# Stage boundaries of a three-layer graph network kernel: who clears the buffers, when a product and a scan start, who stores the last rows

## The reference

```
edge_index = stack([src, dst])
h = maximum(layernorm(x), 0)
x = x + gat(h)                      # 4 heads of 256, self loops, softmax over a node's edges
    # xp = h @ W; e = leaky_relu(a_src[src] + a_dst[dst]); alpha = softmax per target
    # relu(segment_sum(xp[src] * alpha, dst) + bias)
h = maximum(layernorm(x), 0)
x = x + sage2(h)                    # two layers, each:
    # h @ W_self + (segment_sum(h[src], dst) / deg) @ W_neigh + b; relu after the first
```

## Time and profile before

| | us |
|---|---|
| median of 3 runs | 3345.1 (3342.63 to 3353.91) |
| profiled execution | 3346.46 |
| its span | 3344.8 |
| PE busy | 2967.8 (89%) |
| VectorE busy | 2337.4 (70%) |
| ScalarE busy | 1209.0 (36%) |
| GpSimd busy | 1554.0 (46%) |

### The profile page before, as it was taken

One profiled execution on the slowest core, in us unless ns is written; L12 is line 12 of the kernel. 1 busy time (PEld: TensorE's weight loads), 2 busy tenths in 40 slices (PEclk: granted clock), 3 DMA queues, 4 the chain that ended last, 5 costly groups with the idle time before them and its releaser, 6 DMA issues. The chain is left out here.

```text
span 3344.8 us, 64541 instructions
## 1 busy us (share of the span) xinstructions
PE 2967.8 (89%) x20467; PEld 1731.9 (52%) x20467; DVE 2337.4 (70%) x3892; ACT 1209.0 (36%) x2576; POOL 1554.0 (46%) x1534
## 2 busy tenths in 40 slices
PE   4568998499999996999799999997799999997998
PEld 4345665388888885444244444443344444443454
DVE  8787898699999997788466666664455555554343
ACT  3553452588888885444122222222000000001111
POOL 2002232377777773222466666661466656561000
PEclk6788999799999998999899999998899999998999
DMA  3987994498888888777799999994999999996544
GB/s 98 280 274 254 326 354 139 136 324 311 321 305 314 314 317 273 218 218 221 257 345 352 340 351 350 361 358 164 310 350 332 326 346 339 335 356 214 139 134 123
DMA packets 275335, 934.78 MB, mean 279 GB/s; under 512 B 46699, under 2 KB 47719, under 8 KB 275136
## 3 DMA queue, kind: packets, MB, share of 16 engines
q0 software_dynamic: 210560, 713.00, 60.5%
q1 hardware_dynamic: 64576, 219.26, 21.0%
HBM read 852.95 MB, written 130.57 MB: 294 GB/s over the span
## 5 line engine op out<-in xcount | busy, mean ns | idle before, releaser
L1666 PE MATMUL gagg_sum_ps<-gagg_got,gagg_hot_hi 128*128 128x256 f16 x3520 | 591.3, 273 | 78.6 <-ACT gagg_hot_hi L1632 31.3
L1632 ACT ACTIVATE gagg_hot_hi<-gagg_hot,all_mem 128x128 f16<-128x128 f16 x1760 | 538.0, 388 | 138.9 <-DVE gagg_hot L1574 138.9
L1551 POOL DMA_INDIRECT gagg_got<-xs_rows,all_idx x440 | 501.0, 1139 | 179.2 <-issue 132.3
L1726 POOL DMA_INDIRECT agg_got<-h_rows,all_run_idx x415 | 411.8, 992 | 340.1 <-PE agg_sum_ps L1784 198.6
L2072 POOL DMA_INDIRECT agg_got<-h_rows,all_run_idx x415 | 419.1, 1010 | 255.2 <-PE agg_sum_ps L2225 147.7
L1666 PE MATMUL gagg_sum_ps<-gagg_got,gagg_hot_lo 128*128 128x256 f16 x1760 | 481.6, 274 | 0.0
L1758 DVE TENSOR_TENSOR sums_acc<-agg_sum_ps,sums_acc 125x1024 f32 x220 | 269.3, 1224 | 292.3 <-PE agg_sum_ps L1784 290.6
L2136 DVE TENSOR_TENSOR sums_acc<-agg_sum_ps,sums_acc 125x1024 f32 x220 | 269.0, 1223 | 228.8 <-PE agg_sum_ps L2225 227.7
L1784 PE MATMUL agg_sum_ps<-agg_got,agg_hot 128*128 128x512 f16 x1660 | 396.4, 381 | 23.6 <-DMA agg_got<-h_rows,all_run_idx 14.0
L2225 PE MATMUL agg_sum_ps<-agg_got,all_mem 128*128 128x512 f16 x1660 | 392.5, 383 | 24.0 <-DVE all_mem L2106 16.7
L1666 PEld LDWEIGHTS gagg_sum_ps<-gagg_got,gagg_hot_hi 128*128 128x128 f16 x3520 | 329.5, 98 | 122.0 <-ACT gagg_hot_hi L1632 53.3
(11 more groups left out here) (336 smaller groups left out, 4013.2 us busy)
## 6 DMA issues: line engine op xcount, KB each, us to landing
gatw_piece<-slot_rows POOLq DMA_DIRECT2D x56, 512.0 KB, 11.3
split_w<-edg_w_out SPq DMA_DIRECT2D x32, 512.0 KB, 9.4
agg_got<-h_rows,all_run_idx POOLq DMA_INDIRECT x830, 8.0
x_rows<-fin_val POOLq DMA_DIRECT2D x25, 500.0 KB
h_rows<-fin_h POOLq DMA_DIRECT2D x25, 500.0 KB
out_dram<-neigh_rows POOLq DMA_DIRECT2D x25, 500.0 KB
norm_x_sb<-in_x_dram SPq DMA_DIRECT2D x25, 448.0 KB
fin_x_sb<-in_x_dram SPq DMA_DIRECT2D x25, 448.0 KB
```

The lines of the kernel that those rows point to most:

```text
L1551: g.indirect_dma_start(out=got[:, k % R, :], out_offset=None, in_=rows_in[:, :], in_offset=bass.IndirectOffsetOnAxis(ap=idx[:, k:k + 1], a ...
L1632: last = a.activation(hot_hi[:, u % HOTS, h, :], hot[:, u % HOTS, :], ACT.Copy, scale=high_e[:, ds(s, 1), h])
L1666: t.matmul(sum_ps[n % 2][:, h * C:(h + 1) * C], hot_k[:, u % HOTS, h, :], got[:, u % R, part * D + h * C:part * D + (h + 1) * C], start=(u ...
L1726: g.indirect_dma_start(out=got[:, k % R, :], out_offset=None, in_=rows_in[:, :], in_offset=bass.IndirectOffsetOnAxis(ap=run_idx[:, col:col ...
```

## The change

Seven places, with no change to what is computed:

1. `norm`: the scan of the weight slices is spread over the steps 4 to 26, its first loads come after the row tiles 0 to 4, and the slot pieces are asked for when four tiles are normalised.
2. `edg`: the last row tile's two stores go from GpSimd to SyncE, and its low part from GpSimd to VectorE.
3. `gagg`, `agg0`, `agg1`: the odd gather buffers are cleared by VectorE between the one-hots of the first two groups, the even ones by ScalarE, and a gather waits for its own buffer's clear.
4. `fin`: the bias is loaded first, and the clear of `h16` goes from VectorE to GpSimd.
5. `agg1`: row tile i is turned and multiplied in round i + 1.
6. `neigh1`: the weights are loaded in eight strips with a semaphore each.
7. `neigh1`: the last tile's product is made half by half, its first half is finished while PE makes the second, and SyncE stores both.

```diff
 # normalize_x
-                seen_in = [list(range(s * SLICES // STEPS, (s + 1) * SLICES // STEPS)) for s in range(STEPS)]
+                seen_in = [[z for z in range(SLICES) if SEE_FROM + z * (STEPS - SEE_FROM) // SLICES == s] for s in range(STEPS)]   # SEE_FROM = 4
...
-                    for z in range(WSEE):
-                        load_w(z)
                     for n in range(NT):
+                        if n == 1:
+                            for z in range(WSEE):
+                                load_w(z)
...
+                    g.wait_ge(hn_ready, XS)
                     for r in range(PIECE_BUFS):
                         load_pieces(r)
 # edge_scores, SyncE, GpSimd, VectorE
+                    sp.wait_ge(rows_out, LEFT)
+                    sp.dma_start(tiles(xp_rows)[:, NT - 1:NT, :], rows[:, :].unsqueeze(1)).then_inc(last_stored, 16)
+                    sp.wait_ge(rows_lo, LEFT)
+                    sp.dma_start(tiles(xs_rows)[:, NT - 1:NT, :], parts16[:, :].unsqueeze(1)).then_inc(last_stored, 16)
+                    sp.wait_ge(last_stored, 32)
...
-                    for p in range(LEFT - AFTER, LEFT):
+                    for p in range(LEFT - AFTER, LEFT - 1):
                         low(p)
...
+                    v.wait_ge(rows_hi, LEFT)
+                    v.wait_ge(rows_lo, LEFT - 1)
+                    v.tensor_tensor(parts16[:, D:2 * D], rows[:, :], parts16[:, 0:D], ALU.subtract).then_inc(rows_lo, 1)
 # sums_and_product (aggregate and neighbours alike, but for the product)
-                        g.wait_ge(mm_done, k + 1)
+                        if k < R:
+                            g.wait_ge(blank[k % 2], k // 2 + 1)
+                        else:
+                            g.wait_ge(mm_done, k + 1)
...
-                    for k in range(R):
-                        v.memset(got[:, k, :].bitcast(f32), 0.0).then_inc(mm_done, 1)
+                    v.sem_inc(mm_done, R)
                     v.sem_inc(added, 2)
-                    prod.start(v)
...
-                    for g in range(AHEAD):
-                        make_hots(g)
+                    for k in range(1, R, 2):
+                        v.memset(got[:, k, :].bitcast(f32), 0.0).then_inc(blank[1], 1)
+                        if k // 2 < AHEAD:
+                            make_hots(k // 2)
+                    prod.start(v)
...
-                        if i < NT and n == RG - 1:
-                            prod.finish(v, i)
+                        if 1 <= i <= NT and n == RG - 1:
+                            prod.finish(v, i - 1)
...   # ScalarE
+                    for k in range(0, R, 2):
+                        a.activation(got[:, k, :].bitcast(f32), ones[:, 0:1].to_broadcast([P, D]), ACT.Copy, scale=0.0).then_inc(blank[0], 1)
...   # TensorE
-                        if i < NT and n == 0:
-                            prod.turn(t, i)
+                        if 1 <= i <= NT and n == 0:
+                            prod.turn(t, i - 1)
...
-                        if i < NT and 1 <= n < RG - 1:
-                            prod.multiply(t, i, n - 1, RG - 2)
+                        if 1 <= i <= NT and 1 <= n < RG - 1:
+                            prod.multiply(t, i - 1, n - 1, RG - 2)
 # gat_finish
+                    sp.dma_start(bias_sb[:, :], gat_bias.partition_broadcast(P)).then_inc(bias_in, 16)
                     for m in range(NT + LAG):
                         if m < NT:
                             load(m)
-                        if m == 0:
-                            sp.dma_start(bias_sb[:, :], gat_bias.partition_broadcast(P)).then_inc(bias_in, 16)
...   # GpSimd, VectorE
+                    g.memset(h16[:, :, :], 0.0).then_inc(cleared, 1)
...
-                    v.memset(h16[:, :, :], 0.0).then_inc(cleared, 1)
 # project
-                    sp.dma_start(w16[:, :, :], split_w[wi].rearrange("(k p) n -> p k n", p=P)).then_inc(w_loaded, 16)
+                    for k in range(KT):
+                        sp.dma_start(w16[:, k, :], split_w[wi][k * P:(k + 1) * P, :]).then_inc(w_loaded[k], 16)
...   # SyncE, behind its loads
+                    for q in range(2):
+                        sp.wait_ge(half_ready, q + 1)
+                        for a, b in CUTS:
+                            sp.dma_start(rows_out[(NT - 1) * TN + a:(NT - 1) * TN + b, q * HALF:(q + 1) * HALF],
+                                         rows[a:b, (NT - 1) % 2, q * HALF:(q + 1) * HALF]).then_inc(half_stored, 16)
+                    sp.wait_ge(half_stored, 2 * CUT)
...   # TensorE
-                        if early(n, 1):
-                            t.wait_ge(w_loaded, 16)
...
-                        for o, l, r, start, stop in products(out_ps[slot], a_t[slot], w16):
+                        todo = products(out_ps[slot], a_t[slot], w16)
+                        if final(n):
+                            for o, l, r, start, stop in todo[0::2]:
+                                last = t.matmul(o, l, r, start=start, stop=stop)
+                            last.then_inc(half_done, 1)
+                            todo = todo[1::2]
+                        for m, (o, l, r, start, stop) in enumerate(todo):
+                            if early(n, 1) and m % 6 == 0:
+                                t.wait_ge(w_loaded[m // 6], 16)
                             last = t.matmul(o, l, r, start=start, stop=stop)
```

More of the change, by code:

```diff
@@ L899, in project, with final @@
                 post_ready = sem("post_ready")
+                def final(n):
+                    return type(n) is int and n == NT - 1
                 post = sb("post", [TN, 1])
@@ L903, in project @@
                 out_ps = [ps(f"out_ps{i}", [P, D]) for i in range(2)]
-                w_loaded, cleared = sem("w_loaded"), sem("cleared")
+                w_loaded = [sem(f"w_loaded{k}") for k in range(KT)]
+                cleared = sem("cleared")
+                half_done, half_read, half_ready, half_stored = sem("half_done"), sem("half_read"), sem("half_ready"), sem("half_stored")
                 add_loaded = [sem(f"add_loaded{i}") for i in range(2)]
@@ L971, in back @@
                     def back(n, slot, half):
+                        if final(n):
+                            v.wait_ge(add_loaded[slot], 2 * CUT * (half + 1))
+                            for q in range(2):
+                                cols = slice(q * HALF, (q + 1) * HALF)
+                                if q == 0:
+                                    v.wait_ge(half_done, 1)
+                                else:
+                                    v.wait_ge(mm_done, n + 1)
+                                v.scalar_tensor_tensor(rows[:, slot, cols], out_ps[slot][0:TN, cols], post[:, 0:1],
+                                                       rows[:, slot, cols], ALU.mult, ALU.add).then_inc(half_read, 1)
+                                v.wait_ge(half_read, q + 1)
+                                v.tensor_tensor(rows[:, slot, cols], rows[:, slot, cols], more[:, slot, cols], ALU.add).then_inc(half_ready, 1)
+                            return
                         v.wait_ge(mm_done, n + 1)
@@ L1539, in aggregate @@
                 mm_done = sem("mm_done")
+                blank = [sem(f"blank{i}") for i in range(2)]
                 added = sem("added")
@@ L1714, in sums_and_product @@
                 issuing, mm_done, added = sem("issuing"), sem("mm_done"), sem("added")
+                blank = [sem(f"blank{i}") for i in range(2)]
                 seq = [cols for run in runs for cols in run]
                 at = [sum(len(cols) for cols in seq[:g]) for g in range(len(seq) + 1)]
-                assert at[-1] == CHUNKS and len(seq) == GROUPS >= RG * NT
+                assert at[-1] == CHUNKS and len(seq) == GROUPS >= RG * (NT + 1)
                 block = ctx.enter_context(nc.Block())
```

38 lines of the change are left out of this document (28 added, 10 removed).

## The result

The changed kernel takes 3310.5 us (median of 4 runs, 3305.0 to 3318.0), the kernel before 3343.9 (4 runs, 3341.3 to 3353.9): the ratio is 0.9896, with a 95% interval from 0.9867 to 0.9925. Forecast were 3314 and -31.8 us; the difference of the medians is -33.4. The profiled execution of the changed kernel took 3318.0 us around a span of 3316.3, 7.5 above its median; so the profiles alone, span against span, show 28.5.

The account below looks back on a forecast made before the run. PE was taken as the bound, with only its dips between stages able to pay. Terms summed to -31.8 us from 3346.5, giving 3314.7, or 3313.3 on the median's scale; forecast 3314, range 3302 to 3329.

Parts of the forecast that it names:

- Self product a round later: `agg1`: head +13.2, warm start -2.7, tail -20.3, taken as -10 us; bounds -2 and -14.
- So PE is the bound and the gathers follow it: `agg1`: GpSimd waits 198.6 us for PE, PE only 14.0 us for a gather, so PE limits the stage.
- Weight scan later: `norm`: 11.5 us gained at tile 1, less 2.4, 1.5 and a 2.6 stall: -5 us; bounds +1 and -9.
- Last rows of `edg`: End of `edg`: VectorE subtracts and SyncE issues 1.0 us earlier, completion perhaps 1 to 2 more: -2 us.
- `gagg` -4.3: Head of `gagg`: four buffer clears moved to ScalarE shorten VectorE's chain before the first add, -4.3 us.
- `agg0` -1.5: Head of `agg0`: one-hots come earlier, but gather arrivals set the eighth add; -1.5 us, bounds -4 and +0.5.
- (a): Rival: `agg1` head starved, gaining only 2 us; `agg0` clears and `norm` gain dissolve in transfers; 3329 us, chance 0.13.
- Strips -5: `neigh1`: weights in eight strips remove PE's 5.13 us wait before the first product, -5 us.
- Last tile -4: End of `neigh1`: only the second half's two passes and a SyncE store follow PE, -4 us.
- (c): Rival: lagged product empties `agg1`'s eight buffers for good, later chunks pay for gathers; 3357 us, chance 0.05.
- (b): Rival: all edits across the stages reach their better bound, -47.6 us to 3299; chance 0.12.
- (d): Rival: barriers hold the stage ends, so only `agg1`, `norm` and strips count, -20 us to 3326.5; chance 0.13.

Follow-up runs that it names:

- e8: Kernel before with only the product of `agg1` a round later: 3335.0 us, ratio 0.9976 to the kernel before.
- e2: Changed kernel with slot pieces spread, last `norm` stores on SyncE, last `norm` and `edg` stores cut into 112 and 13 rows, nine `agg1` buffers: 3291.5 us.
- e4: Changed kernel with `agg1` row tiles 1 to 24 loaded in 64 of 2048 columns and last `norm` stores on SyncE: 3286.7 us.
- e6: Kernel before with nine gather buffers instead of eight in `agg1`: 3324.1 us, ratio 0.9946 to the kernel before.
- e7: Changed kernel with slot pieces at the start, last `norm` and `edg` stores on SyncE in 112 and 13 rows, nine `agg1` buffers: 3285.3 us.
- e5: Changed kernel with nine `agg1` buffers, product in its own round again, and the `norm` scan as before with pieces still late: 3302.3 us.
- e1: Changed kernel with early slot pieces, GpSimd storing the last `edg` rows, `fin` clear on VectorE, `agg1` product in its own round: 3319.7 us.
- e3: Changed kernel with `agg0` and `agg1` clears all on VectorE before one-hots, last weights in one DMA, slot pieces spread: 3317.5 us.
- e9: Changed kernel with GpSimd storing the last tile's halves, GpSimd subtracting in `edg` with cut SyncE stores, ten `agg0` buffers: 3316.2 us.

## Why the prediction was right, and where it was not

The time was forecast at 3314 and is 3310.5, and the waits that were to go did go. But the closeness is partly luck: five terms missed by 1.4 to 4.1 us, three one way and two the other. The forecast's steps in its order:

- *Self product a round later, -10.* Right in kind; too large by 4.1 in this pair and by 2.9 in e8's. Head: +13.3, as forecast to 0.1 us. Tail: 17.9 gained where 20.3 were forecast. The step "less a little as full buffers start it: 28.5" failed: from the product's end to the end of the last add 30.8 us remained. PE records 2.6 us of waits for gathers there, so the buffers were not full. Rounds: 1.3 gained where 2.7 were forecast for the warm start. That start came, since the 5.3 us at the lower clock are gone from the rounds (2.7 by the estimate above), but two stretches of 3.4 us at the lower clock behind late gathers took back 3.4. Lag against no lag, over all profiles with eight buffers, is (697.8, 694.7, 696.5, 700.9) against (703.7, 709.8); as the rounds scatter, head and tail tell it better, 92.2 to 93.6 against 97.0 and 98.2, that is -3.4 to -6.0 where the forecast had -7.1.
- *What bounds the stage.* "So PE is the bound and the gathers follow it" was half true, and it hid the largest gain that the runs found. The 198.6 us that GpSimd waits for PE and the 14.0 that PE waits for gathers were read as one queue that is always full. It isn't: at some times a gather is late. PE's recorded waits in the rounds are 11.9 us before and 10.8 after, and its busy time also holds lost time: 591 and 590 us, against 584 to 586 in e2, e4, e6 and e7 (589 in e5). About half of that difference is the lower clock. The share of 0.98 in the earlier trace rows looked like a full transfer system, and one more buffer brought 3% more through it (335 to 345 GB/s in the rounds from the kernel before to e6, 338 to 349 from the changed kernel to e2). The sum of the forecast didn't depend on it, since both kernels lose it.
- *Weight scan later, -5.* Measured -1.3 in the profiled pair. From the stage's first DMA to VectorE's last subtraction the profiles of the old code took 169.8, 172.4 and 170.5 us, those of the new 168.8, 169.0 and 166.1: -2.9. What failed is the estimate of the stall, "2.6 us": the late pieces cost 3.6 us by these means and 5.6 from e1 to the changed kernel. And it came by another way than I had named. VectorE waited 1.7 us for slices in all, but ScalarE waited 27.1 us for stores of normalised rows (9.3 before), which the late pieces seem to have pushed. With the pieces at the start, 163.2 and 165.6, -6.5. The later scan is right; the later pieces, the other half of the same edit, took back more than half of it. Spreading them further (171.9 and 172.0) is worse than either. As `edg` itself scatters by 10 us, the two stages together are the safer measure. Without the end of `edg` they took 521.4 to 527.6 us in the old code, 525.6 and 530.6 in the new, and 521.3 and 516.6 with the pieces at the start. So over both stages only e7 is clear of the old code, 2.3 us of it by SyncE's stores, and the gain of the changed kernel can't be told from nothing. Why does it matter when 3 MB move? The likely reason, which no run isolates: at the start nothing else is urgent for the transfer engines, while from 96 to 220 us their share is 0.93 or more in six stretches of seven, so that a megabyte put in there makes something else late.
- *Last rows of `edg`, -2.* Measured -5.9, steady to 0.1 us over profiles. VectorE's subtraction gave 0.9 of the forecast 1.0. "Completion may give 1 to 2 more" failed: I carried over 6.4 us from the end of the span, and this stage needs 12.5 behind a GpSimd issue. The loss by the five engines is real and 3.2 us (1.5 was the estimate), so the gain would have been 9.1 with cut stores.
- *`gagg` -4.3:* right. The first add comes 28.7 us into the stage in the three profiles of the old code and 24.7 in the eight of the new, so 4.0 are sure; the 4.4 of the pair holds a little scatter. *`fin` 0:* right. *`agg0` -1.5:* nothing measurable; PE's 16.7 us wait for one-hots became a 16.3 us wait for the first gather, as rival (a) had it.
- *Strips -5:* -5.1 by e3. *Last tile -4:* -4.7 behind PE's end; the halves gave 1.7 of it and SyncE's queue 3.0. Another 1.1 came between the first product and PE's end (282.4 to 281.3), whose cause is open.

Of the rivals, (a) was half right in `norm` and `agg0` and wrong in `agg1`'s head. (c) didn't come: the rounds took 604.1 and not 648. But a smaller price of late gathers was hiding in both kernels, at 0.8 us a round. (b) did not come: only the ends of `edg` and of the kernel did better than their bounds. The rivals' times stand on the scale of the profiled execution, 1.4 us above that of the forecast, which changes none of this. (d) is refuted, since the ends of `edg` and of the kernel and `gagg` gave 15 us of the 28.5.

What stays open: why `edg` ends 12.5 us after GpSimd's last issue, and `norm` only 6. Also why rounds with the same work and eight buffers differ by up to 11 us between profiles (601.2 to 612.8): about 4.5 of these are the clock, the rest is not explained. And why `edg` without its end scatters by 10 us.

## What to carry to other kernels

A producer that waits long for its consumer does not prove that the consumer never waits: compare the consumer's own pace with a run in which the producer has less to do, and try one more buffer before re-ordering work. When an edit moves two transfers, cost each by what shares the engines at its new time; in `norm` the same 3 MB cost 3.6 to 5.6 us more at 98 us than at the start. End a stage with stores from SyncE, cut so that their rows divide well over the engines, and let GpSimd finish early: e9 shows that the store alone is not enough. Before explaining why two profiles of the same loop differ, look at the granted clock in it.

## What the runs showed of the hardware

- A 125-row store from SyncE in one piece moved at 131 GB/s with a share of 0.32; cut into 112 and 13 rows it peaked at 279 GB/s with 0.94.
- GpSimd as the last worker of a stage costs by the stage: the next stage comes 12.5 us after the end of its last issue in `edg` (in before, e1, e6 and e8 alike), 5.8 to 6.6 in `norm` (eight kernels), and 5.8 passed to the span's end in e9. With SyncE's cut stores it was 4.3 in `edg` (e2, e7) and 3.7 to 4.4 in `norm` (e2, e4, e7).
- In the rounds of `agg1` the granted clock fell to its lower level for 3.4 us ten times in seven kernels, each time within 1.3 us of the end of a wait of PE of 2.0 to 3.3 us for a gather; matmuls then follow each other every 0.43 us instead of 0.22.
- In `fin` GpSimd's clear and VectorE's first instruction start and end together. The latter is a 125 x 25 operation that takes 0.18 us in the kernel before and in e1, where GpSimd clears nothing; here both take 3.5 us:

```profile
1287.80 3.51 POOL L1941 MEMSET fin_h<- 128x4096 f16 x1 [11.20 <-POOLq L121]
1287.84 3.50 DVE L1958 TENSOR_SCALAR all_mem<-sums_acc 125x25 f32<-125x25 f32 x1 [1.51 <-PEq L121]
```

  The Trainium skill, "SBUF — State Buffer", section "SBUF: two separate sides", says that VectorE, in its modes that use two ports, and GpSimd share a pair of ports by an exclusive lock, and that whoever comes second is blocked while the other's instruction lasts. The rows agree with it: GpSimd starts 0.04 us ahead, and VectorE ends 0.03 us behind it. It cost nothing here, as VectorE then waits 3.3 us for row data anyway.
- Something like it shows in `agg0`'s head. GpSimd's gather issues take 1.89, 1.01, 1.81 us while VectorE alternates clears and one-hots, and 1.05, 1.01, 0.99 in e3, where it only clears (there the seventh takes 1.92, beside the first one-hots). The seventh is issued 11.4 us into the stage against 10.1. This works against the shared clears. How much it took from them is not shown: PE starts 10.9 us into the stage, now held by the first gather, where it started at 11.2, held by the one-hots:

```profile
1614.76 1.89 POOL L2140 DMA_INDIRECT agg_got<-h_rows,all_run_idx  x1 [24.92 <-DVE agg_got L2195]
1616.95 1.01 POOL L2140 DMA_INDIRECT agg_got<-h_rows,all_run_idx  x1 [0.30 <-ACT agg_got L2252]
1618.27 1.81 POOL L2140 DMA_INDIRECT agg_got<-h_rows,all_run_idx  x1 [0.30 <-DVE agg_got L2195]
```
